# One clearing of the semaphores at the end, and the last stage's first norm made a stage earlier

## The chip, the cores and the metric

The kernel runs on one core of a Trainium2 chip. The metric is the device time of one execution in microseconds. The median of three timed runs of the kernel before is 1267.13 us (1265.65 to 1269.34).

## What is computed

The input is 16 sequences of 256 tokens with 128 features, so 4096 tokens in 32 tiles of 128. Six layers follow one another, each with a residual and a norm of its own in front:

```python
def _layernorm(x, axis=-1, eps=1e-05):
    m = jnp.mean(x, axis=axis, keepdims=True)
    v = jnp.var(x, axis=axis, keepdims=True)
    return (x - m) / jnp.sqrt(v + eps)
...
    x = x + 0.5 * _L0_ffn_ref(_layernorm(x, axis=-1), ...)
    x = x + _L0_attn_ref(_layernorm(x, axis=-1), ...)
    x = x + 0.5 * _L0_ffn_ref(_layernorm(x, axis=-1), ...)
    x = x + 0.5 * _L1_ffn_ref(_layernorm(x, axis=-1), ...)
    x = x + _L1_attn_ref(_layernorm(x, axis=-1), ...)
    x = x + 0.5 * _L1_ffn_ref(_layernorm(x, axis=-1), ...)
    return x
```

`_L0_ffn` routes every token to two of eight experts, `_L0_attn` is differential attention, `_L1_attn` a linear attention whose state is carried along the tokens by a scan. `_L1_ffn` is a feed-forward layer with quantized weights, and it norms its input a second time (mean, `rsqrt(var + EPS)`) and adds its result to that normed input:

```python
        residual = x
        mu = jnp.mean(x, axis=-1, keepdims=True)
        var = jnp.mean(jnp.square(x - mu), axis=-1, keepdims=True)
        h = (x - mu) * jax.lax.rsqrt(var + EPS) * ln_gamma + ln_beta
...
        return residual + 0.5 * z.reshape(residual.shape)
```

So a token of this layer needs two factors from one variance: that of the first norm alone (`r0`, for the residual) and that of both norms together (`r01`, for `h`).

## The kernel before

All 32 tiles of tokens stay on the chip in one array `x` (`all_x` in the trace, features along the free axis). The work is done in groups of four tiles (TG = 4, 512 tokens), so eight groups (NG = 8). Six stages run one after another, each a function that writes the instruction list of every engine by hand: `sorted_moe` ("moe0"), `diff_attention` ("diff"), `sorted_moe` again ("moe1"), `quantized_ffn` ("ffn0"), `linear_attention` ("lin"), `quantized_ffn` again ("ffn1"). Waits and signals between engines are semaphores that the stage allocates through a `Names` object. When a stage ends, three things happen in a row: the end of its block, a barrier of all engines (its line is that of the stage's `with`); then `Names.clear`, which sets the stage's semaphores back on POOL (line 58, a drain and one ranged clear); then a second barrier of all engines (line 59). There are 13 `Names` objects. Five end at the boundaries between stages, with 79, 78, 81, 19 and 23 semaphores; the other eight (ffn1's and those of weights and shared tiles) end one after another at the end of the kernel.

**Start of diff.** POOL issues eight indirect gathers (lines 2039 and 2031) and then makes the first scale `diff_rstd` (2011) by a power on 128x2 values. DVE normalises with it (`diff_xn`, 2535), PE transposes, ACT rounds the result to fp16 (`diff_xT_hi`, 2223).

**Start of moe1.** Part of its rows has been sorted and scattered during diff. POOL scatters the rest group by group (`exp_xs`, line 468), waiting for the row numbers that DVE makes.

**lin's rounds.** A round treats one group in eight steps f = 0 to 7, each for an eighth of the state. For even f DVE multiplies `lin_kv` from PSUM (line 3080), for odd f POOL does it from SBUF (2932). DVE scans (`lin_state`, 3093), POOL multiplies the state with the queries (`lin_y`, 2945), PE projects (`lin_o_ps`, 3164). At f = 5 DVE adds the projected result of the group before to `x` (`add_out`, 3099). Rounds up to the sixth also prepare a later group; the last round prepares nothing, and behind it `add_out` of the last group ends the stage.

**ffn1's start.** For group 0 DVE computes statistics (1539, 1543) and two variances (1546 for both norms, 1548 for the first), POOL raises them to the power -1/2 (`r01` at 1453, `r0` at 1457), DVE normalises four tiles (`ffn_hn`, 1565), PE transposes (1649), ACT and DVE split the result in two fp16 parts (1494, 1571), PE multiplies with the weights (1659 up, 1672 down). Group 1's statistics come behind the split of group 0 on DVE. On POOL an addition of the bias to `x` (1462, 128x512) follows each group's powers; DVE's `ffn_keep` and `ffn_shift` (1557, 1558) make the residual's factors for ACT (1507).

Of the kernel before, what the change touches and what calls it, by code (L numbers as in the profile page):

```python
# [15 lines left out]
P = 128  # L16
# [95 lines left out]
class ExpertWeights:  # L112


    def __init__(self, nc, ctx, w, tiles):
# [4 lines left out]
        nm = Names(nc, ctx, "exp")  # L120
# [48 lines left out]
def sorted_moe(nc, tag, x, ident, neghalf, made, ew, first_layer, fetched_here, x_in=None, later=None, deq=None, ahead=0, fetch=None, begin=None):  # L169
# [75 lines left out]
    with ExitStack() as ctx:  # L245
        nm = Names(nc, ctx, tag)
# [103 lines left out]
        dest_ready = nm.sem("dest_ready")  # L350
        zeroed = nm.sem("zeroed")
        spare_in = nm.sem("spare_in")
# [12 lines left out]
        fetched = [nm.sem(f"fetched{i}") for i in range(YG)]  # L365
        tile_in = [nm.sem(f"tile_in{t}") for t in range(TG)]
        x_added = nm.sem("x_added")
        fetch_used = nm.sem("fetch_used")
        s_g = nm.sem("s_g")
        s_u = nm.sem("s_u")  # L370
        s_act = nm.sem("s_act")
        s_h = nm.sem("s_h")
        s_hi = nm.sem("s_hi")
        s_lo = nm.sem("s_lo")
        s_done = nm.sem("s_done")
        s_added = nm.sem("s_added")
        w1_ready = nm.sem("w1_ready")
        deq_own = nm.sem("deq_own")
# [76 lines left out]
        def _(pool):  # L455
# [810 lines left out]
class Fetched:  # L1266


    def __init__(self, nc, ctx):
        nm = Names(nc, ctx, "fetched")  # L1270
        self.yg = nm.sb("yg", [P, FETCH_RING, TG, 2, P], F32)
        self.come = [nm.sem(f"come{i}") for i in range(FETCH_RING)]
# [2081 lines left out]
```

## Time and profile before

| | us |
|---|---|
| median of three timed runs | 1267.13 |
| the profiled execution, its own time | 1273.58 |
| its span in the trace | 1271.8 |
| PE busy in the span | 1018.7 (80%) |
| DVE busy | 864.3 (68%) |
| ACT busy | 659.8 (52%) |
| POOL busy | 650.0 (51%) |

The stages end at about 230, 773, 971, 1042, 1199 and 1268 us of the span. In the trace a timeline row gives start, duration, engine, line, operation, tile written and tiles read, and in brackets the idle time of the engine before it and what ended that. A row of a line without timeline gives the number of instructions, the shortest, median and longest duration in nanoseconds, and the first and last start. PEclk is the granted clock of TensorE, where 1.00 is 2.4 GHz and 0.50 is 1.2 GHz.

### The profile page before, as it was taken

Reading aid. Unit: us, or ns where it says so; the run is one execution under the profiler, and the core shown is the slowest. Engines: PE = TensorE matmul, PEld = TensorE weight load, DVE = VectorE, ACT = ScalarE, POOL = GpSimd, SP = SyncE. Lnnn points to the kernel's source line nnn. Section 1 sums busy time; section 2 is a strip of 40 time slices with the busy share of each in tenths; the row PEclk is TensorE's granted clock in tenths of the full one; section 3 lists DMA queues with packets and bytes.
Section 4 is the critical chain, followed back from the end, with each engine's and each line's share of the span. In section 5 each row is a group of like instructions: output and inputs, shape, how many; then the busy total and the mean of one; then the engine's idle time right before and its main releaser. Section 6 shows DMA issues by size and latency. Waiting matters only on the chain. (4 is left out here: it accounts for less than half of the span.)

```text
span 1271.8 us, 30703 instructions
## 1 busy us (share of the span) xinstructions
PE 1018.7 (80%) x10960; PEld 750.0 (59%) x10992; DVE 864.3 (68%) x2321; ACT 659.8 (52%) x1248; POOL 650.0 (51%) x697
## 2 busy tenths in 40 slices
PE   3646699778999889898889875787874989999697
PEld 1434588346766666566666644666663765666466
DVE  7645678556887878686868636675556956778672
ACT  4622466536677667576756543343443644444173
POOL 5754300465556576657563334355552316888751
PEclk9868799789999989899999886898887998999999
DMA  8212343134443343334343313422213000000001
GB/s 241 75 45 57 110 115 94 38 56 69 63 58 55 54 67 58 62 57 68 54 62 50 55 27 108 116 74 71 60 36 112 33 1 2 1 1 1 1 26 42
DMA packets 279667, 75.50 MB, mean 59 GB/s; under 512 B 217152, under 2 KB 273504, under 8 KB 279136
## 3 DMA queue, kind: packets, MB, share of 16 engines
q1 hardware_dynamic: 270528, 53.43, 22.2%
q0 software_dynamic: 8992, 20.11, 5.0%
q8 instruction: 92, 1.51, 0.5%
q14 instruction: 55, 0.45, 0.1%
HBM read 28.08 MB, written 24.17 MB: 41 GB/s over the span
## 5 line engine op out<-in xcount | busy, mean ns | idle before, releaser
L2333 DVE TENSOR_REDUCE diff_peak<-diff_s_ps 128x2 f16<-128x384 f32 (+7 forms) x384 | 208.4, 558 | 111.0 <-PE diff_s_ps L2597 74.0
L2183 ACT ACTIVATE diff_prob<-diff_st_ps 128x512 f32<-128x512 f32 x320 | 187.6, 596 | 123.0 <-PE diff_st_ps L2619 97.5
L2619 PE MATMUL diff_st_ps<-diff_qT,diff_k_pair 128*128 128x256 f16 (+3 forms) x1024 | 127.5, 237 | 8.3 <-issue 6.3
L2597 PE MATMUL diff_s_ps<-diff_kT,diff_q_block 128*128 128x32 f16 (+7 forms) x1024 | 132.1, 231 | 1.8 <-issue 1.8
L492 POOL DMA_INDIRECT exp_ys<-moe_y_sb,moe_dest x78 | 78.4, 1005 | 82.9 <-ACT moe_y_sb L578 63.0
L2635 PE MATMUL diff_ot_ps<-diff_prob,diff_v 128*32 128x256 f32 (+3 forms) x2048 | 113.7, 314 | 0.6 <-ACT diff_prob L2183 0.4
L571 ACT ACTIVATE moe_h_hi<-moe_h 128x512 f16<-128x512 f32 x94 | 59.2, 630 | 103.2 <-DVE moe_h L894 90.5
L2594 PE MATMUL diff_s_ps<-diff_mask,diff_ident_bf 128*128 128x64 bf16 (+1 forms) x384 | 79.9, 208 | 31.1 <-DVE diff_peak L2333 20.9
L894 DVE TENSOR_TENSOR moe_h<-moe_act,moe_u_ps 128x512 f32<-128x512 f32 x94 | 64.2, 683 | 45.8 <-remote 20.1
L2945 POOL TENSOR_TENSOR lin_y<-lin_state,lin_qT 128x512 f32<-128x512 f32 x64 | 81.2, 1268 | 15.6 <-DVE lin_state L3093 12.9
L565 ACT ACTIVATE moe_act<-moe_g_ps 128x512 f32<-128x512 f32 x94 | 55.4, 590 | 64.0 <-remote 37.4
L3093 DVE TENSOR_TENSOR_SCAN lin_state<-lin_lam_ps,lin_kv 128x512 f32<-128x512 f32 x64 | 76.6, 1215 | 10.4 <-POOL lin_kv L2932 8.0
L3164 PEld LDWEIGHTS lin_o_ps<-last_lin_wo,lin_y 128*128 128x128 f32 x512 | 65.0, 191 | 26.8 <-POOL lin_y L2945 21.5
L468 POOL DMA_INDIRECT exp_xs<-moe_xh,exp_rows x64 | 64.7, 1010 | 27.8 <-issue 18.3
L3164 PE MATMUL lin_o_ps<-last_lin_wo,lin_y 128*128 128x128 f32 x512 | 70.3, 280 | 10.6 <-POOL lin_y L2945 10.6
L2619 PEld LDWEIGHTS diff_st_ps<-diff_qT,diff_k_pair 128*128 128x128 f16 x1024 | 70.2, 100 | 9.8 <-issue 5.0
L889 DVE TENSOR_TENSOR moe_h_lo<-moe_h,moe_h_hi 128x512 f16<-128x512 f32 x94 | 65.0, 692 | 13.5 <-ACT moe_h_hi L571 9.8
L2615 PE MATMUL diff_st_ps<-diff_mask_T,diff_ident_bf 128*128 128x128 bf16 (+1 forms) x288 | 67.3, 234 | 8.3 <-ACT diff_prob L2183 5.8
L2594 PEld LDWEIGHTS diff_s_ps<-diff_mask,diff_ident_bf 128*128 128x128 bf16 x384 | 38.1, 99 | 59.6 <-DVE diff_peak L2333 44.2
L1140 PE MATMUL moe_g_ps<-moe_xgT,exp_up_hi 128*128 128x256 f16 x312 | 61.0, 291 | 15.3 <-DVE moe_xgT L875 12.9
L2635 PEld LDWEIGHTS diff_ot_ps<-diff_prob,diff_v 128*32 128x32 f32 x2048 | 52.3, 111 | 31.7 <-issue 12.1
L2597 PEld LDWEIGHTS diff_s_ps<-diff_kT,diff_q_block 128*128 128x128 f16 x1024 | 64.5, 101 | 5.8 <-issue 3.8
(438 smaller groups left out, 3035.3 us busy)
## 6 DMA issues: line engine op xcount, KB each, us to landing
moe_xg<-exp_xs SPq DMA_DIRECT2D x78, 130.0 KB, 2.3
diff_q_block<-diff_qT SPq DMA_DIRECT2D x128, 64.0 KB
diff_k_pair<-diff_kT SPq DMA_DIRECT2D x128, 64.0 KB
exp_y_slots<-moe_y_sb SPq DMA_DIRECT2D x39, 128.0 KB, 2.0
diff_v_new<-diff_v_raw SPq DMA_DIRECT2D x64, 64.0 KB
fetched_yg<-exp_ys SPq DMA_DIRECT2D x7, 512.0 KB, 4.0
all_x<-in_x SPq DMA_DIRECT2D x4, 512.0 KB, 5.4
moe_up<-in_w SPq DMA_DIRECT2D x16, 128.0 KB, 3.5
```

The source lines that it names most:

```text
L492: nc.gpsimd.indirect_dma_start(out=ew.ys, out_offset=bass.IndirectOffsetOnAxis(ap=dest[:, s, j:j + 1], axis=0), in_=y_sb[:, s % YR, j], in ...
L889: nc.vector.tensor_tensor(h_lo[:, i % HR], h[:, i % 2], h_hi[:, i % HR], ALU.subtract).then_inc(lo_ready, 1)
L2183: nc.scalar.activation(prob[:, n % RING], st_ps[:, e % 2], ACT.Exp, scale=SCALE).then_inc(exp_ready, 1)
L2333: nc.vector.tensor_reduce(peak[:, half, c0:c0 + n, i], s_ps[:, u % 2, 0:n * wd].rearrange("p (c k) -> p c k", k=wd), op=ALU.max, axis=AX.X ...
L2594: nc.tensor.matmul(out[:, :, wd - QB:], ident_bf[:], mask[:, 0:n], start=True, stop=False, skip_group_check=True)
L2597: last = nc.tensor.matmul(out[:, c], q_block[:, ch, i].rearrange("p r q -> p (r q)"), kT[:, B % 2, ch, 0:wd], start=False, stop=True, skip ...
L2615: nc.tensor.matmul(cols, ident_bf[:], mask_T[:, 0:len(equal)], start=True, stop=False, skip_group_check=True)
L2619: last = nc.tensor.matmul(out[:, at:at + wd], k_pair[:, h % 2, h // 2, i].rearrange("p r k -> p (r k)"), qT[:, C % 3, h // 2, KB * i:S], s ...
L2635: last = nc.tensor.matmul(ot_ps[32 * r:32 * r + 32, half, col:col + wd], v[:, b % 2, i, h], prob[:, (b * EXPS + n) % RING, at:at + wd], st ...
L2945: nc.gpsimd.tensor_tensor(y[:, f % RING], state[:, f % STATES], qT[:, b], ALU.mult).then_inc(y_ready, 1)
L3093: nc.vector.tensor_tensor_scan(state[:, f % STATES], lam_ps[:, b], kv[:, f % RING], 0.0, ALU.mult, ALU.add).then_inc(state_ready, 1)
L3164: last = nc.tensor.matmul(o_ps[:, b, t * P:(t + 1) * P], y[:, f % RING, t * P:(t + 1) * P], wo[:, f], start=(f == 0 and t == 0), stop=(f = ...
```

## The change

Two things are done. First, `Names` takes a list and no longer clears: the barrier at a block's end stays, line 58's clear and line 59's barrier go from all 13 places. The semaphores of moe0 (67 now) are cleared by POOL inside diff, behind the eight gathers and ahead of the first `diff_rstd`; those of diff (78) by POOL inside moe1, between two scatters. All others (70 and 66, in two ranges) are cleared once at the end of the kernel, with one barrier behind. So that enough semaphores are left, the moe stages no longer allocate those that they don't use. Second, the norm of ffn1's group 0 and the statistics of its group 1 move into lin's last round: the tiles and semaphores are a new object `FfnNorm`, handed to both stages as `opening`. They work on groups 0 and 1 of `x`, which lin has finished rounds earlier.

```diff
 class Names:
-    def __init__(self, nc, ctx, prefix):
+    def __init__(self, nc, ctx, prefix, sems):
         self.nc, self.ctx, self.prefix = nc, ctx, prefix
-        self.sems = []
-        ctx.callback(self.clear)
-
-    def clear(self):
-
-        self.nc.clear_and_free_semaphores(self.sems)
-        self.nc.all_engine_barrier()
+        self.sems = sems
...
# sorted_moe, POOL
                 scatter(ahead - 1, EARLY + 1)
+                nc.clear_and_free_semaphores(spent)
                 scatter(ahead)
...
# quantized_ffn, POOL
-            scale_both(0)
-            scale_first(0)
+            if not opened:
+                scale_both(0)
+                scale_first(0)
...
# quantized_ffn, DVE
-            statistics(0)
-            normalise(0)
+            if not opened:
+                statistics(0)
+                normalise(0)
             add_results(1, 0)
             low(0)
             add_results(1, 1)
-            statistics(1)
+            if not opened:
+                statistics(1)
             scales(0)
...
# diff_attention, POOL
                     gather(1, n)
+            if spent:
+                nc.clear_and_free_semaphores(spent)
             scale_of(0)
...
# linear_attention, POOL
+                    if f == 5 and opening and not prepares:
+                        pool.wait_ge(opening.both_var_ready, 1)
+                        nc.gpsimd.tensor_tensor(opening.r01[:, 0], opening.var[:, 0, 0], neghalf[:, 0:TG], ALU.pow).then_inc(opening.r01_ready, 1)
             pairs(pool, group)
+            if opening:
+                pool.wait_ge(opening.var_ready, 1)
+                nc.gpsimd.tensor_tensor(opening.r0[:, 0], opening.var[:, 0, 1], neghalf[:, 0:TG], ALU.pow).then_inc(opening.r0_ready, 1)
...
# linear_attention, DVE
+                    if opening and not prepares and f == 4:
+                        opening_statistics(0)
...
             pairs(dve, group)
+            if opening:
+                opening_normalise()
+                opening_statistics(1)
             add_out(NG - 1, 1)
...
# build
+        nc.clear_and_free_semaphores(sems)
+        nc.all_engine_barrier()
```

`opening_statistics(g)` is the four BN_STATS, four BN_AGGR and two variances of lines 1539 to 1548 on group g; `opening_normalise()` the four instructions of line 1565 on group 0, which wait for `r01`.

DVE from the middle of lin's last round to ffn1's first work. `lin_state` is the scan, `all_x<-all_x,lin_o_ps` is `add_out`, the branches are the change of stage. Before:

```order
L3080 TENSOR_TENSOR lin_kv<-lin_v_ps,lin_kT 128x512
L3093 SCALAR_TENSOR_TENSOR lin_state<-lin_lam_ps,lin_kv 128x512 x2
L3099 TENSOR_TENSOR all_x<-all_x,lin_o_ps 128x512
L3080 TENSOR_TENSOR lin_kv<-lin_v_ps,lin_kT 128x512
L3093 SCALAR_TENSOR_TENSOR lin_state<-lin_lam_ps,lin_kv 128x512 x3
L3099 TENSOR_TENSOR all_x<-all_x,lin_o_ps 128x512
L2852 UNCONDITIONAL_BRANCH
L1520 UNCONDITIONAL_BRANCH
L1539 BN_STATS ffn_stats<-all_x 128x6 x4
L1543 BN_AGGR ffn_mv<-ffn_stats 128x2 x4
L1546 TENSOR_SCALAR ffn_var<-ffn_mv 128x4
L1548 TENSOR_SCALAR ffn_var<-ffn_mv 128x4
```

The same stretch of DVE now, from the scan of f = 3 to the last `add_out`; names with `open_` are the new object's tiles:

```order
L3109 SCALAR_TENSOR_TENSOR lin_state<-lin_lam_ps,lin_kv 128x512
L3120 BN_STATS open_stats<-all_x 128x6 x4
L3124 BN_AGGR open_mv<-open_stats 128x2 x4
L3127 TENSOR_SCALAR open_var<-open_mv 128x4
L3129 TENSOR_SCALAR open_var<-open_mv 128x4
L3109 SCALAR_TENSOR_TENSOR lin_state<-lin_lam_ps,lin_kv 128x512
L3115 TENSOR_TENSOR all_x<-all_x,lin_o_ps 128x512
L3096 TENSOR_TENSOR lin_kv<-lin_v_ps,lin_kT 128x512
L3109 SCALAR_TENSOR_TENSOR lin_state<-lin_lam_ps,lin_kv 128x512 x3
L3134 TENSOR_SCALAR open_hn<-all_x,open_mv,open_r 128x128 x4
L3120 BN_STATS open_stats<-all_x 128x6 x4
```

Group 0's statistics stand ahead of the scan of f = 4, and group 0's normalisation and group 1's statistics between the last scan and the last `add_out`.

POOL from lin's last steps into ffn1, before (`L58 ISA` is the ranged clear):

```order
L2945 TENSOR_TENSOR lin_y<-lin_state,lin_qT 128x512 x2
L2932 TENSOR_TENSOR lin_kv<-lin_v_sb,lin_kT 128x512
L2945 TENSOR_TENSOR lin_y<-lin_state,lin_qT 128x512 x2
L2852 UNCONDITIONAL_BRANCH
L58 ISA
L1449 UNCONDITIONAL_BRANCH
L1453 TENSOR_TENSOR ffn_r<-ffn_var,all_neghalf 128x4
L1457 TENSOR_TENSOR ffn_r<-ffn_var,all_neghalf 128x4
```

and now:

```order
L2955 TENSOR_TENSOR lin_y<-lin_state,lin_qT 128x512 x2
L2960 TENSOR_TENSOR open_r<-open_var,all_neghalf 128x4
L2942 TENSOR_TENSOR lin_kv<-lin_v_sb,lin_kT 128x512
L2955 TENSOR_TENSOR lin_y<-lin_state,lin_qT 128x512 x2
L2965 TENSOR_TENSOR open_r<-open_var,all_neghalf 128x4
L2862 UNCONDITIONAL_BRANCH
L1454 UNCONDITIONAL_BRANCH
L1458 TENSOR_TENSOR open_r<-open_var,all_neghalf 128x4
```

The power for `r01` stands ahead of the last `lin_kv`, that for `r0` behind the last `lin_y`, and the clear is gone.

POOL at diff's start, now (before, the clear stood ahead of the gathers, in a place of its own between the stages):

```order
L2047 DMA diff_prob<-exp_y_slots,exp_places 128x128 x4
L2039 DMA diff_yg<-exp_y_slots,exp_places 128x128 x4
L2077 ISA
L2019 TENSOR_TENSOR diff_rstd<-diff_var,all_neghalf 128x2
L2080 MEMSET diff_k_pack 128x64
```

The clear of moe0's semaphores has moved behind the last gather, directly ahead of the first scale.

## Rows read from the trace of the kernel before

**Rows 1.** Lines 58, 59 at moe0's end: count, ns min/median/max, starts in us.

```profile
L58 POOLq DRAIN  x1: 184/184/184, 230.1 to 230.1; - x1
L58 POOLq EVENT_SEMAPHORE_RANGE_CLEAR  x1: 463/463/463, 230.4 to 230.4; - x1
...
L59 ACTq EVENT_SEMAPHORE  x1: 17/17/17, 231.1 to 231.1; - x1
```

**Rows 2.** The same two lines at lin's end.

```profile
L58 POOLq DRAIN  x1: 77/77/77, 1199.1 to 1199.1; - x1
...
L59 ACTq EVENT_SEMAPHORE  x1: 17/17/17, 1199.6 to 1199.6; - x1
```

**Rows 3.** Line 59 in the last four microseconds of the kernel.

```profile
L59 ACTq EVENT_SEMAPHORE  x8: 17/17/17, 1268.8 to 1271.7; - x8
```

**Rows 4.** Timeline at diff's start: start, us, engine, line, operation, idle before.

```profile
241.80 0.73 POOL L2011 TENSOR_TENSOR diff_rstd<-diff_var,all_neghalf 128x2 f32<-128x2 f32 x1
...
243.72 0.38 ACT L2223 ACTIVATE diff_xT_hi<-diff_m_ps 128x256 f16<-128x256 f32 x1 [0.67 <-PE diff_m_ps L2716]
```

**Rows 5.** diff's end on POOL: a DMA in the timeline, its landing, the drain.

```profile
771.30 0.95 POOL L2136 DMA_INDIRECT exp_xs<-exp_xh,exp_rows  x1 [0.30 <-issue]
...
exp_xs<-exp_xh,exp_rows POOLq DMA_INDIRECT x2, 2.3
...
L58 POOLq DRAIN  x1: 163/163/163, 772.9 to 772.9; - x1
```

**Rows 6.** Timeline in moe1, POOL, the scatter behind the place of the clear.

```profile
788.16 0.95 POOL L468 DMA_INDIRECT exp_xs<-exp_xh,exp_rows  x1 [4.82 <-DVE exp_rows L683]
```

**Rows 7.** Timeline of lin's last round, DVE and POOL.

```profile
1186.38 2.34 DVE L3093 TENSOR_TENSOR_SCAN lin_state<-lin_lam_ps,lin_kv 128x512 f32<-128x512 f32 x2
...
1190.22 2.34 DVE L3093 TENSOR_TENSOR_SCAN lin_state<-lin_lam_ps,lin_kv 128x512 f32<-128x512 f32 x2
...
1194.05 1.22 DVE L3093 TENSOR_TENSOR_SCAN lin_state<-lin_lam_ps,lin_kv 128x512 f32<-128x512 f32 x1 [1.49 <-POOL lin_kv L2932]
...
1192.75 1.27 POOL L2932 TENSOR_TENSOR lin_kv<-lin_v_sb,lin_kT 128x512 f32<-128x512 f32 x1
1193.98 2.64 POOL L2945 TENSOR_TENSOR lin_y<-lin_state,lin_qT 128x512 f32<-128x512 f32 x2
...
1197.87 0.69 DVE L3099 TENSOR_TENSOR all_x<-all_x,lin_o_ps 128x512 f32<-128x512 f32 x1 [2.60 <-PE lin_o_ps L3164]
```

**Rows 8.** Timeline of ffn1's start, DVE, POOL and PE.

```profile
1199.69 0.87 DVE L1539 BATCH_NORM_STATS2 ffn_stats<-all_x 128x6 f32<-128x128 f32 x4 [1.14 <-PEq L59]
...
1201.26 1.01 POOL L1453 TENSOR_TENSOR ffn_r<-ffn_var,all_neghalf 128x4 f32<-128x4 f32 x1 [4.64 <-DVE ffn_var L1546]
1202.24 1.01 POOL L1457 TENSOR_TENSOR ffn_r<-ffn_var,all_neghalf 128x4 f32<-128x4 f32 x1
1202.31 1.11 DVE L1565 TENSOR_SCALAR ffn_hn<-all_x,ffn_mv,ffn_r 128x128 f32<-128x128 f32 x4 [1.05 <-POOL ffn_r L1453]
...
1203.48 1.11 PE L1649 MATMUL ffn_t_ps<-all_ident,ffn_hn 128*128 128x128 f32 x4 [5.64 <-DVE ffn_hn L1565]
...
1206.01 0.61 PE L1659 MATMUL ffn_y_ps<-ffn_hT_hi,deq_fc_hi 128*128 128x512 f16 x1 [1.41 <-DVE ffn_hT_lo L1571]
...
1211.81 0.66 PE L1649 MATMUL ffn_t_ps<-all_ident,ffn_hn 128*128 128x128 f32 x4 [3.06 <-DVE ffn_hn L1565]
```

**Rows 9.** Timeline in ffn1, four normalisations of DVE beside POOL's bias addition.

```profile
1220.38 2.11 DVE L1565 TENSOR_SCALAR ffn_hn<-all_x,ffn_mv,ffn_r 128x128 f32<-128x128 f32 x4
...
1221.14 1.26 POOL L1462 TENSOR_TENSOR all_x<-all_x,last_bias 128x512 f32<-128x512 f32 x1 [0.94 <-ACT all_x L1507]
```

**Rows 10.** Windows: stretch, length, busy PE, PEld, DVE, ACT, POOL, PEclk, DMA.

```profile
970.60:991.00 20.40, 9.68 (x26) 4.15 (x27) 16.84 (x81) 6.79 (x14) 6.16 (x6) 0.50 0.30 96
...
1199.10:1216.58 17.48, 8.63 (x26) 3.42 (x27) 10.47 (x51) 6.72 (x14) 7.19 (x7) 0.71 0.00 0
1216.58:1265.58 49.00, 48.24 (x359) 39.57 (x358) 25.29 (x94) 30.11 (x59) 18.84 (x17) 1.00 0.13 39
```

More of the change, by code:

```diff
@@ L166, in load_consts, with sorted_moe @@
         sp.dma_start(self.own_row[:], w["own_row"]).then_inc(self.consts_in, 16)
-def sorted_moe(nc, tag, x, ident, neghalf, made, ew, first_layer, fetched_here, x_in=None, later=None, deq=None, ahead=0, fetch=None, begin=None):
+def sorted_moe(nc, tag, x, ident, neghalf, made, ew, first_layer, fetched_here, x_in=None, later=None, deq=None, ahead=0, fetch=None, begin=None, sems=None, spent=()):
     w = ew.w
@@ L364, in sorted_moe @@
         y_stored = [nm.sem(f"y_stored{i}") for i in range(YR)]
[L365 to L375, printed above, removed]
+        fetched = [nm.sem(f"fetched{i}") for i in range(YG if fetched_here else 0)]
+        tile_in = [nm.sem(f"tile_in{t}") for t in range(TG if fetched_here else 0)]
+        x_added = nm.sem("x_added") if fetched_here else None
+        fetch_used = nm.sem("fetch_used") if fetched_here else None
+        s_g = nm.sem("s_g") if not ahead else None
+        s_u = nm.sem("s_u") if not ahead else None
+        s_act = nm.sem("s_act") if not ahead else None
+        s_h = nm.sem("s_h") if not ahead else None
+        s_hi = nm.sem("s_hi") if not ahead else None
+        s_lo = nm.sem("s_lo") if not ahead else None
+        s_done = nm.sem("s_done") if not ahead else None
         s_added = nm.sem("s_added")
-        w1_ready = nm.sem("w1_ready")
-        deq_own = nm.sem("deq_own")
+        w1_ready = nm.sem("w1_ready") if deq else None
+        deq_own = nm.sem("deq_own") if deq else None
         block = ctx.enter_context(nc.Block(no_gpsimd_drain=True))
@@ L1313, with __init__ @@
 class LastWeights:
-    def __init__(self, nc, ctx, w):
+    def __init__(self, nc, ctx, w, sems):
         self.w = w
@@ L1372, with __init__ @@
 class NextNorm:
-    def __init__(self, nc, ctx, tiles, done):
-        nm = Names(nc, ctx, "next")
+    def __init__(self, nc, ctx, tiles, done, sems):
+        nm = Names(nc, ctx, "next", sems)
         self.done = done
@@ L3222, in build @@
     NG = T // TG
+    sems, moe0_sems, diff_sems = [], [], []
     with ExitStack() as ctx:
-        nm = Names(nc, ctx, "all")
+        nm = Names(nc, ctx, "all", sems)
         x = nm.sb("x", [P, T + TG, P], F32)
@@ L3266, in _ @@
                     last.load(sp)
-        norm = NextNorm(nc, ctx, T, NG - 2 if "d" in phases else 0)
+        norm = NextNorm(nc, ctx, T, NG - 2 if "d" in phases else 0, sems)
         if "d" in phases:
-            quantized_ffn(nc, "ffn0", x, ident, neghalf, made, dequantized, None, None, experts if fetch else None, fetch, norm)
+            quantized_ffn(nc, "ffn0", x, ident, neghalf, made, dequantized, sems, None, None, experts if fetch else None, fetch, norm)
+        opening = FfnNorm(nc, ctx, "open", sems) if "e" in phases and "f" in phases else None
         if "e" in phases:
-            linear_attention(nc, "lin", x, ident, neghalf, made, last, norm)
+            linear_attention(nc, "lin", x, ident, neghalf, made, last, norm, opening, sems)
         if "f" in phases:
-            quantized_ffn(nc, "ffn1", x, ident, neghalf, made, dequantized, out_tiles, stored)
+            quantized_ffn(nc, "ffn1", x, ident, neghalf, made, dequantized, sems, out_tiles, stored, opened=opening)
         else:
```

123 lines of the change are left out of this document (74 added, 49 removed).

## The prediction

> **What bounds the kernel now.** No engine bounds the whole span, so I read the places that the change touches, each by what ends its wait last. First the two lines of the clear and its barrier. At moe0's end the clear's drain begins at 230.1 and the other engines are let go at 231.1, of which 0.46 us are the ranged clear of 79 semaphores [rows 1]: 1.0 us in which nobody works. The boundaries diff to moe1 and moe1 to ffn0 have 78 and 81 semaphores and read alike, 0.9 us each. At lin's end it is 0.5 us (1199.1 to 1199.6) for 23 semaphores [rows 2], and the same at ffn0's end for 19. At the kernel's end eight of them follow one another: the first lets go at 1268.8, the last at 1271.7, so 2.9 us for seven, 0.41 each, 3.3 us for eight [rows 3]. All 13 together are 7.1 us. They are on the path by construction: behind each the first work of every engine waits for line 59, as DVE does at ffn1's start [rows 8].
>
> Then ffn1's start. From the last `add_out` of lin (1197.87, [rows 7]) to the first multiplication with weights (1206.01) there is a chain of one engine after another: statistics 1199.69, powers 1201.26, normalisation 1202.31, transposes 1203.48 [rows 8]. PE then waits 3.06 us once more, for group 1's normalisation, until 1211.81 [rows 8]. From 1216.58 to 1265.58 PE is busy 48.24 of 49.00 us at the full clock [rows 10], so what is gained ahead of that stretch arrives at the end one for one. In the 17.48 us before it the granted clock is 0.71 on average [rows 10], that is 10.1 us at 1.2 GHz and 7.4 at 2.4 GHz.
>
> Last, the place that takes over the work. In lin's last round POOL is the engine that sets the pace: `lin_kv` 1192.75, two `lin_y` from 1193.98 to 1196.62, back to back, while DVE idles 1.49 us ahead of its last scan and 2.60 us ahead of `add_out` [rows 7].
>
> **Boundaries.** moe0 to diff: 1.0 us go, but the clear comes back inside diff on POOL, behind the last gather, and `diff_rstd` starts there with no idle time [rows 4]: POOL is late already. 67 semaphores by 0.463/79 give 0.39 us, and from the drain's start to the clear's it is 0.3 [rows 1], so `diff_rstd` comes 0.7 later in its stage. DVE, PE and ACT hang on it (ACT's rounding has 0.67 us of idle before it, ended by PE, [rows 4]). Net 0.3. Bounds: 1.0 if other waits hide POOL's clear, and 0.3 - 1.35 = -1.0 if its drain waits until the last gather has landed (2.3 us from its issue, of which the issue itself is 0.95, [rows 5]). Against the second: at diff's end the drain took 0.163 us at 772.9 [rows 5], while a DMA issued at 771.30 would land at 773.6. I take 0.3.
>
> diff to moe1: 0.9 go. The clear of 78 semaphores, 0.3 + 0.46 = 0.8 us, stands where POOL then waits 4.82 us for DVE [rows 6]; that wait hides it, and without it 0.8 would be back. moe1 to ffn0: 0.9. ffn0 to lin: 0.5. Both stages begin with work that waits on line 59 alone. Bounds for each: nothing to the full amount; I take the full amount, 2.3 together, since the barrier's release is what ended the first wait.
>
> Kernel's end: 3.3 us become two drains and ranged clears and one barrier: 0.1 + 70 x 5.9 ns, 0.1 + 66 x 5.9 ns, and a barrier of 1.0 - 0.3 - 0.46 = 0.24 [rows 1], 1.25 us in all. That is a gain of 2.05, of which I take 2.0; bounds 1.6 (drains of 0.3, as at moe0's end) and 2.2.
>
> **lin's last round gets longer.** Four steps. (1) Statistics of group 0 take DVE 1201.26 - 1199.69 = 1.57 us [rows 8], ahead of the scan of f = 4; they move the scan of f = 5 from 1190.22 [rows 7] to about 1191.6 (a little less than 1.57, since DVE waited for PE ahead of it) and its result from 1191.5 to 1192.8. The `lin_y` of f = 5, which POOL began right after the one before, starts about 1.2 us later. (2) The power for `r01` takes POOL 1.0 us [rows 8], ahead of the last `lin_kv`: 1192.75 becomes 1195.0. The last scan starts at 1196.3 instead of 1194.05, and the last `lin_y` runs from 1197.55 to 1198.85, 2.2 us later than before. (3) DVE has finished its last scan at about 1197.4 and should normalise (1.11 us) and make group 1's statistics (1.57), done by 1200.1; PE's projection is done at 1198.85 + 1.2 = 1200.05 (1196.62 to 1197.87 before, [rows 7]). The two would just fit, and `add_out` would be 2.2 us late. (4) But the normalisation runs beside POOL's last `lin_y`. In ffn1 there is a row for just that: four normalisations that take 1.11 us alone [rows 8] took 2.11 when POOL's 128x512 addition began between them [rows 9], ending only when POOL's did; POOL's was not longer. I take the same here: the normalisation stands still until 1198.85, ends at 1199.9, the statistics at 1201.4, and `add_out` starts at 1201.4, 3.5 us late. Bounds 2.2 (no hold) and 4.5 (the power for `r0`, 1.0 us, that POOL starts behind the last `lin_y`, holds it too).
>
> The Trainium skill, page "SBUF — State Buffer", section "SBUF: two separate sides", states that DVE in a two-port mode and GpSimd share one pair of ports as an exclusive lock that the first holds for its whole instruction while the other stands still. The row of the 2.11 us agrees. By the letter of that rule the power would hold DVE as well; the trace doesn't agree: the normalisation of 1202.31 ran beside the power of 1202.24 in its usual 1.11 us [rows 8]. By the rule the sum would be 1.0 us worse, by the row it is as above.
>
> **ffn1's start gets shorter.** Behind `add_out` (0.69) the block's barrier takes 1199.1 - 1198.56 = 0.5 [rows 2, 7], then PE can transpose at once: 1201.4 + 0.7 + 0.5 + 0.1 = 1202.7. From transposes to the first multiplication it is 1206.01 - 1203.48 = 2.5 [rows 8]: 1205.2, a gain of 0.8 against 1206.01 (the boundary's 0.5 is in it). The multiplications of group 0 lasted 1211.81 - 3.06 - 1206.01 = 2.74 us. Group 1's powers now follow from 1202.6 on POOL, two by 1.0 [rows 8], DVE splits until 1205.2, makes the residual's factors and normalises until about 1206.8; PE wants group 1 at 1205.2 + 2.7 = 1207.9. So the wait of 3.06 us goes, and 3.9 are gained. On the clock: if all of PE's 8.63 us of work in that stretch [rows 10] was at half speed, at most 4.3 more can come back. One idle stretch of PE ahead of the transposes stays (1200.05 to 1202.7), the other goes; I take 1.2, nearer to nothing. Together 5.1, bounds 3.9 - 1.0 (longer hold) and 8.2.
>
> **The sum.** 0.3 + 0.9 + 0.9 + 0.5 + 2.0 + 5.1 = 9.7 us. The profiled execution would go from 1273.58 to 1263.9; the median of the timed runs lies 6.45 us (0.5%) below it, and with the same difference 1267.13 becomes 1257.4. A measurement of this kernel tells a change from none at about 0.3%, 3.8 us.
>
> **Rivals.**
> (a) No hold at lin's end: DVE slips its four normalisations in ahead of the last `lin_y` or beside it. 1.3 less, 1256.1. For it: the two start within 0.15 us of each other. Against: the row of 2.11 us.
> (b) The clock doesn't fall at ffn1's start, because PE's idle time there is 2.6 instead of 5.6 us: up to 4.3 - 1.2 = 3.1 more, 1254.3. Against: the wait of 3.06 us was long enough to be followed by some of the 10.1 us at half speed.
> (c) The power holds DVE as well: 1.0 more, 1258.4. Against: the 1.11 beside 1202.24.
> (d) The change does not do what it says: the boundaries' time is only moved, because each stage's first long wait is for a DMA or for POOL's clear (the drain in diff waits for its gathers). Then -1.0 stands for 0.3 and nothing for 2.3: 3.6 less, 1261.0. Against: the first waits end at line 59.
> (e) Slower: the earlier start of ffn1 falls into a long stretch of half clock. ffn0 has one, 20.40 us at 0.50 with PE busy only 9.68 us [rows 10], ended only after PE had become busy. In ffn1 PE is the bound, so every us at half speed costs 0.5. My forecast leaves some 7 us at half; from 7 + 2 x 9.7 = 26 us the gain is gone, from 34 the kernel is slower by 0.3%, and with 40 us it takes 1257.4 + 16.5 = 1274. Against: before, with more idle time, the clock was back for good by 1216.58 [rows 10].
>
> **How the numbers follow.** Forecast 0.41, (a) 0.22, (b) 0.13, (c) 0.05, (d) 0.12, (e) 0.07. Predicted is the likeliest, 1257.4. The range goes from 1252.0, below (a) and (b), to 1262.5, beyond (d) by its unknown drain; what is left out is (e) and the ends of (b) and (d). Faster by over 0.3% (below 1263.3) are the forecast, (a) to (c) and most of (d): 0.91. Within 0.3%: the rest of (d), 0.02, and the shorter stretches of (e), 0.04: 0.06. Slower: 0.03.
>
> **What would show it.** In the profile after: no line 58 and 59 at the boundaries, one pair of clears in the last 1.3 us; in diff a gap of 0.7 us ahead of the first `diff_rstd`; in lin's last round the last `lin_kv` at about 2.2 us later behind the round's start, `open_hn` longer than 1.11 us for four, and `add_out` some 3.5 us later; in ffn1 no wait of PE for group 1's normalisation. The prediction is wrong if the drain in diff takes more than a microsecond, if PE still waits around group 1, or if the granted clock stays at 0.5 for more than 10 us in ffn1.

## The result, and the profile after

The changed kernel was timed three times against the kernel before, 20, 12 and 12 runs: 1258.32, 1262.54 and 1265.47 us in the median against 1266.17, 1272.2 and 1270.9. The ratios are 0.9947 (95% interval 0.9928 to 0.9966), 0.9922 (0.9896 to 0.9948) and 0.9940 (0.9909 to 0.9971): between 0.3 and 1.0% faster, with the best guess near 0.6%, or 7.9 us by the first pair of medians. Forecast were 1257.4 us and a gain of 9.7. One execution scatters by several us (1252.7 to 1266.5 in the first series), so terms of a microsecond can't be read from times. They can be read from the traces by stage.

The table takes, for each profiled execution, the time from the last signal of one stage's end barrier to that of the next (for the kernels that clear between stages, from the end of that clearing's barrier); the last column runs from there to the end of the kernel. The kernels other than before and changed are those of the experiments below; the record counts the profiled execution of the late clear as slow, so its ratio below is that of its five others. moe0, diff and moe1 scatter by 7, 13 and 5 us between kernels whose code there is alike; ffn0, ffn1 and the end repeat within 0.1 to 0.6 us.

| profile | moe0 | diff | moe1 | ffn0 | lin | ffn1 | end |
|---|---|---|---|---|---|---|---|
| before | 229.5 | 541.8 | 197.8 | 69.7 | 156.3 | 68.7 | 3.4 |
| changed | 226.2 | 548.9 | 197.0 | 69.7 | 159.8 | 61.0 | 1.5 |
| changed, second | 229.4 | 539.1 | 196.6 | 69.6 | 159.7 | 60.9 | 1.5 |
| changed, third | 228.4 | 542.9 | 199.9 | 69.7 | 159.8 | 60.9 | 1.5 |
| clears only | 233.6 | 536.3 | 198.2 | 69.2 | 155.5 | 69.3 | 1.5 |
| opening only | 230.3 | 538.6 | 196.9 | 69.1 | 158.1 | 60.9 | 3.8 |
| late clear | 232.7 | 545.2 | 200.7 | 69.2 | 159.6 | 60.9 | 1.5 |
| norm on ACT | 229.3 | 546.3 | 196.6 | 69.5 | 159.8 | 60.9 | 1.5 |
| early norm | 230.8 | 542.9 | 200.3 | 69.3 | 156.4 | 63.1 | 1.5 |
| early norm, second | 227.8 | 536.6 | 199.3 | 69.3 | 156.3 | 63.1 | 1.5 |
| three groups | 230.9 | 538.7 | 195.8 | 69.2 | 155.4 | 59.3 | 1.5 |
| three groups, second | 229.0 | 546.2 | 199.8 | 69.7 | 156.6 | 59.3 | 1.5 |
| one power more | 228.1 | 543.0 | 200.7 | 69.3 | 158.2 | 60.4 | 1.5 |

lin scatters by up to 1.3 us, because its first scan comes 12.1 to 12.4 us behind the stage's start in three profiles (clears only, opening only, the first of three groups) and 13.6 us in all others, whatever the change. Its last round doesn't scatter like that. From that round's first scan (at 1180.72 before, 1180.69 in the changed kernel) to the stage's end it takes 18.33 us before and 21.58 in the changed kernel, and where its code is the same the profiles agree within 0.02, with one exception that opening only shows.

The profiled execution of the changed kernel took 1266.52 us (span 1264.7), 7.06 less than that of before. Its clears, by line (count, ns shortest, median, longest, first and last start): inside diff, inside moe1, and two at the end with the one barrier that is left.

```profile
L2077 POOLq DRAIN  x1: 7115/7115/7115, 230.5 to 230.5; - x1
L2077 POOLq EVENT_SEMAPHORE_RANGE_CLEAR  x1: 398/398/398, 237.7 to 237.7; - x1
...
L495 POOLq DRAIN  x1: 6809/6809/6809, 778.7 to 778.7; - x1
L495 POOLq EVENT_SEMAPHORE_RANGE_CLEAR  x1: 457/457/457, 785.5 to 785.5; - x1
...
L3324 POOLq DRAIN  x2: 134/140/146, 1263.3 to 1263.9; - x2
L3324 POOLq EVENT_SEMAPHORE_RANGE_CLEAR  x2: 392/402/413, 1263.4 to 1264.1; - x2
...
L3325 ACTq EVENT_SEMAPHORE  x1: 17/17/17, 1264.7 to 1264.7; - x1
```

Lines 58 and 59 are gone from the boundaries. The drains of 7.1 and 6.8 us are not work: POOL's sequencer reaches the drain early and holds it while the gathers or scatters in front of it run. What counts is when the ranged clear is through.

Timeline of diff's start in the changed kernel, to be held against [rows 4]:

```profile
236.54 0.94 POOL L2039 DMA_INDIRECT diff_yg<-exp_y_slots,exp_places  x1 [0.30 <-issue]
238.19 0.72 POOL L2019 TENSOR_TENSOR diff_rstd<-diff_var,all_neghalf 128x2 f32<-128x2 f32 x1 [0.71 <-issue]
...
238.95 1.33 DVE L2545 TENSOR_SCALAR diff_xn<-all_x,diff_mv,diff_rstd 128x128 f32<-128x128 f32 x2 [1.05 <-POOL diff_rstd L2019]
239.09 1.11 POOL L2055 TENSOR_TENSOR diff_yg<-diff_yg,exp_gate 128x512 f32<-128x512 f32 x1
...
241.06 0.38 ACT L2233 ACTIVATE diff_xT_hi<-diff_m_ps 128x256 f16<-128x256 f32 x1 [2.24 <-PE diff_m_ps L2726]
```

The gap ahead of `diff_rstd` is the 0.7 that was forecast. Not forecast is the next line: DVE's two normalisations took 1.33 us together and not 0.60, as in the kernel before:

```profile
242.56 0.60 DVE L2535 TENSOR_SCALAR diff_xn<-all_x,diff_mv,diff_rstd 128x128 f32<-128x128 f32 x2 [0.59 <-POOL diff_rstd L2011]
```

POOL's weighting of the gathered rows (`diff_yg`) began at 239.09, while the first of them ran; the second began at 239.21 and ended at 240.28, just behind the weighting.

Timeline of lin's last round and ffn1's start in the changed kernel, the lines that answer to [rows 7] and [rows 8]:

```profile
1193.77 1.01 POOL L2960 TENSOR_TENSOR open_r<-open_var,all_neghalf 128x4 f32<-128x4 f32 x1
...
1194.74 1.26 POOL L2942 TENSOR_TENSOR lin_kv<-lin_v_sb,lin_kT 128x512 f32<-128x512 f32 x1
1195.96 2.66 POOL L2955 TENSOR_TENSOR lin_y<-lin_state,lin_qT 128x512 f32<-128x512 f32 x2
...
1197.17 2.04 DVE L3134 TENSOR_SCALAR open_hn<-all_x,open_mv,open_r 128x128 f32<-128x128 f32 x4
1197.28 3.78 PE L3206 MATMUL lin_o_ps<-last_lin_wo,lin_y 128*128 128x128 f32 x16 [2.26 <-POOL lin_y L2955]
...
1201.10 0.69 DVE L3115 TENSOR_TENSOR all_x<-all_x,lin_o_ps 128x512 f32<-128x512 f32 x1 [0.41 <-PE lin_o_ps L3206]
...
1202.37 1.09 PE L1657 MATMUL ffn_t_ps<-all_ident,open_hn 128*128 128x128 f32 x4 [1.31 <-PEq L2862]
...
1204.87 0.61 PE L1667 MATMUL ffn_y_ps<-ffn_hT_hi,deq_fc_hi 128*128 128x512 f16 x1 [1.42 <-DVE ffn_hT_lo L1577]
```

The four normalisations took 2.04 us beside POOL's last product, about the 2.11 that were forecast. But the line of the last addition says what it waited for: 0.41 us for PE, whose last 16 projections took 3.78 us. The windows of the changed kernel (stretch, length, busy time of PE, PEld, DVE, ACT, POOL, then PEclk, DMA share and GB/s) show why:

```profile
1180.00:1196.00 16.00, 12.28 (x82) 9.20 (x82) 12.48 (x22) 1.79 (x3) 14.66 (x13) 1.00 0.00 2
1196.00:1209.40 13.40, 9.40 (x33) 6.42 (x34) 9.41 (x36) 4.10 (x8) 8.03 (x9) 0.50 0.00 0
1209.40:1216.00 6.60, 6.60 (x45) 4.78 (x44) 3.78 (x18) 6.21 (x13) 3.90 (x4) 0.98 0.00 0
1216.00:1260.00 44.00, 43.76 (x326) 35.70 (x324) 21.71 (x83) 26.64 (x52) 15.65 (x14) 1.00 0.15 43
```

PE had idled 2.26 us for POOL's delayed `lin_y`, and the granted clock was at 0.50, which is 1.2 GHz, from 1196.1 to 1209.7, already inside lin. Before, PE's last eight projections took 1.16 us and the clock was full to the stage's end:

```profile
1196.67 1.16 PE L3164 MATMUL lin_o_ps<-last_lin_wo,lin_y 128*128 128x128 f32 x8 [0.22 <-POOL lin_y L2945]
...
1189.00:1199.00 10.00, 6.61 (x46) 5.13 (x43) 5.24 (x6) 0.60 (x1) 7.39 (x6) 1.00 0.00 0
```

### The profile page after: what moved, and what is told of

The parts are those of the page before. It is cut to its first block and busy times, and to the rows that moved or that the text cites. A ratio compares the mean times of both kernels' runs of the same rounds, so it can differ in the third digit from the quotient of the medians.

```text
span 1264.7 us, 30585 instructions
## 1 busy us (share of the span) xinstructions
PE 1026.6 (81%) x10992; PEld 753.3 (60%) x10992; DVE 865.5 (68%) x2321; ACT 660.1 (52%) x1248; POOL 649.1 (51%) x697
## 5 line engine op out<-in xcount | busy, mean ns | idle before, releaser
L2645 PE MATMUL diff_ot_ps<-diff_prob,diff_v 128*32 128x256 f32 (+3 forms) x2048 | 116.3, 315 | 2.9 <-issue 2.5
L2625 PE MATMUL diff_st_ps<-diff_mask_T,diff_ident_bf 128*128 128x128 bf16 (+1 forms) x320 | 79.9, 250 | 8.5 <-issue 6.2
```

The source lines that it names most:

```text
L2625: nc.tensor.matmul(cols, ident_bf[:], mask_T[:, 0:len(equal)], start=True, stop=False, skip_group_check=True)
L2645: last = nc.tensor.matmul(ot_ps[32 * r:32 * r + 32, half, col:col + wd], v[:, b % 2, i, h], prob[:, (b * EXPS + n) % RING, at:at + wd], st ...
```

## Experiments

Theory: the change is two independent halves; the boundaries and the end give what their barriers took, less the clear in diff; lin's end is set by DVE standing still beside POOL. Two rivals for the 2 us by which the measured gain is smaller than the forecast: diff itself becomes longer (548.9 against 541.8), or that is scatter.

**Clears only** (the changed kernel, ffn1 makes its own first norm):

```diff
-        opening = FfnNorm(nc, ctx, "open", sems) if "e" in phases and "f" in phases else None
+        opening = None
```

> The changed kernel with the first half of the change alone: no clears between stages, but ffn1 makes its own first norm again. Theory: the two halves are separate and add up. lin's stage takes 156.3 us from release to release as before, ffn1's 68.7 us as before, the five boundaries (3.9 us by the trace) and 2.0 us of the kernel's end are gone, and 1.5 us come back at diff's start, where the clear delays the first scale by 0.6 and DVE's second normalisation then stands still beside POOL's weighting. Together 4.4 us faster than before, about 1262. Rival 1: the clear costs diff much more than that (diff took 548.9 us in the changed kernel's profile, 541.8 before); then diff is near 549 here as well and little is gained. Rival 2: these 7 us are scatter between executions; then diff lies anywhere from 540 to 550 with and without the clear.

Measured: 0.9982 of the kernel before (0.9955 to 1.0009; 12 runs). lin 155.5 and ffn1 69.3 us, the end 1.5, and diff 536.3 with the clear ahead of the scale. So the clear doesn't lengthen diff by 7 us, and rival 1 falls. The expected gain of 4.4 us would be a ratio of 0.9965; that lies inside the interval, and so does no gain at all, so the times show neither.

**Opening only** (the clears and barriers between stages as before; `Names` clears again, the clears in diff, moe1 and at the end are taken out):

```diff
 class Names:
-        self.sems = sems
+        self.sems = []
+        ctx.callback(self.clear)
```

> The second half alone: every stage clears its semaphores behind a barrier of its own again, and ffn1's first norm is made in lin's last round (the object of that norm adds one clear of 0.4 us at the end). Theory: lin takes 159.8 us (3.5 longer than before) and ffn1 61.0 (7.7 shorter), so 4.2 - 0.4 = 3.8 us faster than before, about 1262.5. In diff the first scale comes 10.7 us behind the release and the two normalisations take 0.60, as before. Rival 1 (the clear in diff costs 7 us): diff takes 542 here. Rival 2 (scatter): diff lies anywhere from 540 to 550.

Measured: 0.9953 (0.9919 to 0.9986; 12 runs). ffn1 60.9 us: this half alone brings ffn1 down by 7.8. lin took 158.1 and not 159.8. Of the 1.7, 1.3 are its early start (136.9 us to the last round's first scan, 138.2 in the changed kernel), and 0.3 the last round itself, 21.26 in place of 21.58. There PE waited the same 2.26 us, but the clock was full through the first eight projections and at half only in the second eight:

```profile
1192.03 1.16 PE L3209 MATMUL lin_o_ps<-last_lin_wo,lin_y 128*128 128x128 f32 x8 [2.26 <-POOL lin_y L2958]
...
1193.43 2.08 PE L3209 MATMUL lin_o_ps<-last_lin_wo,lin_y 128*128 128x128 f32 x8 [0.24 <-POOL lin_y L2958]
```

DVE was through with its statistics at 1195.44 and PE with the projections at 1195.51, so here the two nearly tie. diff took 538.6 without any clear in it, within the scatter of those with one. In diff's start the two normalisations took 0.60 us, with POOL's weighting behind them:

```profile
243.20 0.60 DVE L2548 TENSOR_SCALAR diff_xn<-all_x,diff_mv,diff_rstd 128x128 f32<-128x128 f32 x2 [0.38 <-POOL diff_rstd L2024]
244.00 1.05 POOL L2060 TENSOR_TENSOR diff_yg<-diff_yg,exp_gate 128x512 f32<-128x512 f32 x1
```

**Late clear in diff** (the changed kernel):

```diff
-            if spent:
-                nc.clear_and_free_semaphores(spent)
             scale_of(0)
...
                     if A is not None:
+                        if spent and A == 0 and u == 9:
+                            nc.clear_and_free_semaphores(spent)
```

> The changed kernel with one thing moved: POOL clears moe0's semaphores not ahead of the first scale but where it waits some 4 us for DVE's first rotary products. Theory: the clear is then hidden; the first scale comes 10.7 us behind the stage's release (11.35 in the changed kernel), the two normalisations take 0.60 together (1.33), ACT's first rounding comes 12.7 behind the release (14.2), so 1.5 us are gained on the changed kernel, about 1256.8. Rival: the clear is hidden where it stands, ACT's three fills set the start of the stage; then the first rounding stays at 14.2.

Measured: 0.9893 (0.9852 to 0.9934; 5 runs). The first scale came 10.66 us behind the stage's release, the normalisations took 0.60 together, ACT's first rounding came 12.56 behind it (14.22 in the changed kernel): theory right, 1.66 us gained at this place. That the ratio is 0.5% below the changed kernel's first one, which is more than that, rests on five runs and on diff's scatter, and the intervals overlap. The early norm, three groups and one power more have the same late clear, with the scale at 10.67 to 10.83 and the rounding at 12.57 to 12.74; the timeline of the early norm shows it:

```profile
242.30 0.74 POOL L2021 TENSOR_TENSOR diff_rstd<-diff_var,all_neghalf 128x2 f32<-128x2 f32 x1
243.08 0.60 DVE L2547 TENSOR_SCALAR diff_xn<-all_x,diff_mv,diff_rstd 128x128 f32<-128x128 f32 x2 [0.59 <-issue]
244.00 1.05 POOL L2057 TENSOR_TENSOR diff_yg<-diff_yg,exp_gate 128x512 f32<-128x512 f32 x1
```

**Norm on ACT.** To see whether DVE's standstill sets lin's end, the normalisation at lin's end goes to ACT:

```diff
# linear_attention, ACT
             pairs(a, group)
+            if opening:
+                a.wait_ge(opening.shift01_ready, 1)
+                for t in range(TG):
+                    last = nc.scalar.activation(opening.hn[:, t], x[:, t], ACT.Identity,
+                                                bias=opening.shift01[:, t:t + 1], scale=opening.r01[:, 0, t:t + 1])
...
# linear_attention, DVE
-                    last = nc.vector.tensor_scalar(opening.hn[:, t], x[:, t], opening.mv[:, 0, t, 0:1], opening.r01[:, 0, t:t + 1],
-                                                   ALU.subtract, ALU.mult)
+                nc.vector.scalar_tensor_tensor(opening.shift01[:], opening.mv[:, 0, :, 0], -1.0, opening.r01[:, 0],
+                                               ALU.mult, ALU.mult).then_inc(opening.shift01_ready, 1)
```

> The changed kernel with one thing moved: the normalisation of ffn1's group 0 at lin's end is made by ACT (with one small product of mean and factor on DVE) instead of by DVE, so that nothing of it stands still beside POOL's last product. Theory: in the changed kernel DVE was done 0.4 us before TensorE's projection, which ran at 1.2 GHz because POOL had been delayed and TensorE had idled; so DVE's statistics end 1.9 us earlier, the last addition waits for TensorE instead, and lin stays at 159.4 to 159.8 us. Rival: DVE's standstill sets lin's end; then lin takes 1.3 us less, 158.5.

Measured (one execution): lin 159.75 us, against 159.77. Its timeline at lin's end:

```profile
1197.17 3.78 PE L3212 MATMUL lin_o_ps<-last_lin_wo,lin_y 128*128 128x128 f32 x16 [2.26 <-POOL lin_y L2957]
1197.24 1.65 ACT L3042 ACTIVATE open_hn<-all_x,open_shift,open_r 128x128 f32<-128x128 f32 x4 [5.77 <-DVE open_shift L3141]
...
1198.51 0.17 DVE L3137 TENSOR_SCALAR open_var<-open_mv 128x4 f32<-128x4 f32 x1
...
1200.99 0.69 DVE L3123 TENSOR_TENSOR all_x<-all_x,lin_o_ps 128x512 f32<-128x512 f32 x1 [2.30 <-PE lin_o_ps L3212]
```

DVE was done at 1198.7 and then waited 2.30 us for PE. The slow projections set lin's end; the standstill is real and was hidden behind them.

**Early norm** (norm on ACT, late clear, and the statistics and powers of the opening spread over rounds with slack; rounds of 17.74 us had been equally long with and without another norm's statistics and power):

```diff
# linear_attention, POOL
-                    if f == 5 and opening and not prepares:
+                    if f == 4 and opening and g == 3:
                         pool.wait_ge(opening.both_var_ready, 1)
...
+                    if f == 4 and opening and g == 6:
+                        pool.wait_ge(opening.var_ready, 1)
...
# linear_attention, DVE
-                    if opening and not prepares and f == 4:
+                    if opening and g == 3 and f == 4:
                         opening_statistics(0)
+                    if opening and g == 6 and f == 4:
+                        opening_statistics(1)
+                    if opening and g == 3 and f == 6:
+                        opening_normalise()
```

Behind the first condition stands the power for `r01`, behind the second that for `r0`, which was made behind the last round; `opening_normalise` is now the small product of mean and factor.

> The changed kernel with the late clear in diff, and with ffn1's first norm spread over rounds of lin in which DVE and POOL have slack: statistics of group 0 and the power for both norms in the fourth round, those of group 1 and the power for the first norm in the seventh, and the normalisation of group 0 on ACT at the end of the last round. Theory: the rounds of 17.74 us do not get longer (rounds with and without another norm's statistics and power were equally long), lin takes 156.3 us again instead of 159.8, ffn1 61 us or, if TensorE's clock stays up through the shorter idle time, down to 59; with 1.5 us from diff's start that is 5 us faster than the changed kernel, about 1253. Rival: what bounds lin's end is something else (TensorE at half clock), and lin stays near 159.

Measured: 0.9895 (0.9863 to 0.9927; 6 runs). lin is back at 156.4 us and its last round at 18.33, so the rounds did hide the work. ffn1 came out at 63.1, not 59 to 61. Timeline of lin's end and ffn1's start, and windows of ffn1's start:

```profile
1196.62 1.16 PE L3213 MATMUL lin_o_ps<-last_lin_wo,lin_y 128*128 128x128 f32 x8 [1.29 <-POOL lin_y L2957]
...
1198.01 1.16 PE L3213 MATMUL lin_o_ps<-last_lin_wo,lin_y 128*128 128x128 f32 x8 [0.22 <-POOL lin_y L2957]
...
1200.48 0.63 PE L1659 MATMUL ffn_t_ps<-all_ident,open_hn 128*128 128x128 f32 x4 [1.31 <-PEq L2864]
...
1207.92 2.10 DVE L1573 TENSOR_SCALAR open_hn<-all_x,open_mv,open_r 128x128 f32<-128x128 f32 x4
...
1208.67 1.26 POOL L1469 TENSOR_TENSOR all_x<-all_x,last_bias 128x512 f32<-128x512 f32 x1 [0.94 <-ACT all_x L1515]
...
1210.07 0.66 PE L1659 MATMUL ffn_t_ps<-all_ident,open_hn 128*128 128x128 f32 x4 [1.91 <-DVE open_hn L1573]
```

```profile
1200.37:1207.37 7.00, 4.56 (x24) 2.23 (x25) 4.58 (x20) 5.33 (x12) 4.89 (x5) 1.00 0.00 0
1207.37:1214.37 7.00, 5.09 (x22) 3.11 (x21) 5.09 (x22) 4.84 (x11) 3.62 (x4) 0.76 0.00 0
```

PE waited 1.29 us for POOL at lin's end, and the transposes took 0.63 us instead of 1.09: the clock stayed at full through lin's end. PE then ran so far ahead that it waited 1.91 us for the third normalisation, which stood still beside POOL's bias addition, and the clock fell after that wait.

The same kernel once more, beside the changed kernel on one chip:

> The changed kernel once more, for a second profile of it and for a comparison on one chip with the other kernels of this call. Theory: lin 159.8 and ffn1 61.0 us as in the first profile, the kernel's end 1.5; moe0 and diff anywhere within some 8 us of their first values. Against the kernel before 0.993 to 0.995. Rival: diff's 548.9 us are the change's doing; then diff is near 549 again.

> The kernel with the norm spread over lin's rounds and the late clear in diff once more, beside the changed kernel on one chip: lin 156.4 and ffn1 63.1 us as in its first profile, so 1.3 us less than the changed kernel from the two, and 1.5 us less at diff's start; ratio to the changed kernel 0.996 to 0.998. If the gain of over 5 us that its first timing suggested is real, the ratio is below 0.996, and something outside these places has become faster.

Measured: the changed kernel 0.9922, the early norm 0.9874 (0.9832 to 0.9916), so about 0.995 of the changed kernel with intervals that overlap. lin and ffn1 account for 1.2 us and diff's start for some 1.8 of the 5.9 between the medians; where the rest comes from, or whether it is there at all, stays open. diff took 539.1 us in the changed kernel this time and 536.6 in the other: the 548.9 of the first profile were scatter.

**Three groups** (early norm, and lin also makes both powers of group 1 and the statistics of group 2; the rings of the norm's tiles get three places):

```diff
# linear_attention, DVE
+                if opening and not prepares:
+                    opening_statistics(2)
                 scan(g, b, NF - 1)
# quantized_ffn, POOL
-            scale_both(1)
-            scale_first(1)
+            if not opened:
+                scale_both(1)
+                scale_first(1)
+            else:
+                scale_both(2)
+                scale_first(2)
```

> As the kernel with the early norm, and lin also makes the powers of group 1 and the statistics of group 2 (in its last round, where DVE waits 1.5 us for POOL's last product), so that ffn1's third normalisation no longer waits for a chain in which POOL's bias addition holds DVE twice. Theory: TensorE's wait of 1.9 us for group 2 goes, with it the 3.2 us at half clock that followed (1.6), lin stays at 156.4 to 156.6, and ffn1 takes 63.1 - 3.5 = 59.6 us; about 6 us faster than the changed kernel. Rival: the wait only moves to group 3, the clock falls then, and ffn1 stays near 63.

Measured: 0.9860 (0.9824 to 0.9897; 6 runs), ffn1 59.3 us. Windows of its start, 7 us each, and the rest:

```profile
1190.67:1197.67 7.00, 4.57 (x24) 2.23 (x25) 3.43 (x15) 5.33 (x12) 3.25 (x3) 1.00 0.00 0
1197.67:1204.67 7.00, 7.00 (x51) 5.47 (x50) 5.58 (x20) 5.75 (x14) 4.53 (x4) 1.00 0.00 0
1204.67:1245.67 41.00, 41.00 (x307) 33.73 (x306) 20.34 (x76) 25.41 (x49) 14.33 (x13) 1.00 0.16 46
```

PE is busy throughout from the second window on, at the full clock. The rival (the wait moves to the next group) falls.

**One power more.** Which delay makes the clock fall at lin's end, that of the statistics on DVE or that of the power on POOL? To the early norm one power on POOL is added where the changed kernel has its own; the result is overwritten later:

```diff
+                    if f == 5 and opening and not prepares:
+                        nc.gpsimd.tensor_tensor(opening.r0[:, 1], opening.var[:, 0, 0], neghalf[:, 0:TG], ALU.pow)
```

> The kernel with the early norm, plus one thing: POOL makes one power more (128x4, its result is overwritten later) ahead of the last product of values and keys in lin's last round, where the changed kernel has one. This measures what that power alone does to TensorE's clock at lin's end. Theory: TensorE's wait for POOL's seventh product grows from 1.3 to 2.3 us, the granted clock falls to 0.5 there as in the changed kernel, so lin grows by 1.0 for the power and about 1.2 for the two projections at half speed, 158.5 us, and ffn1 begins at half clock and takes 61 us. Rival: the fall needs the delayed scan as well (the statistics on DVE ahead of it); then lin takes 157.4 us and the clock stays at 1.00 until ffn1.

Measured (one execution): lin 158.2, 1.8 to 1.9 us longer than the early norm for a power of 1.01. Timeline and window at lin's end:

```profile
1191.75 1.01 POOL L2964 TENSOR_TENSOR open_r<-open_var,all_neghalf 128x4 f32<-128x4 f32 x1
...
1195.27 3.48 PE L3215 MATMUL lin_o_ps<-last_lin_wo,lin_y 128*128 128x128 f32 x16 [2.26 <-POOL lin_y L2957]
1198.78 0.69 DVE L3125 TENSOR_TENSOR all_x<-all_x,lin_o_ps 128x512 f32<-128x512 f32 x1 [3.53 <-PE lin_o_ps L3215]
```

```profile
1193.95:1199.95 6.00, 3.48 (x16) 3.29 (x16) 1.91 (x2) 0.00 (x0) 2.52 (x3) 0.72 0.00 0
```

The power alone does it: PE's wait grows from 1.29 to 2.26 us, the clock falls, and 16 projections take 3.48 us. The rival (it needs the delayed scan as well) falls. Other than expected, the clock was at full again when ffn1 began and fell 1.8 us later. The last comparison on one chip:

> The changed kernel a third time, for the comparison of this call: lin 159.7, ffn1 60.9, the end 1.45 us; 0.992 to 0.995 of the kernel before.

> The kernel with three groups' statistics made in lin once more, beside the changed kernel: lin 155.4 to 156.4, ffn1 59.3 us, so about 5.5 us less than the changed kernel from the two and 1.5 less at diff's start; 0.985 to 0.989 of the kernel before and 0.993 to 0.996 of the changed kernel.

Measured: the changed kernel 0.9940 (0.9909 to 0.9971), three groups 0.9881 (0.9835 to 0.9926). In both comparisons three groups take 0.994 of the changed kernel's ratio; by stages it is 159.8 + 60.9 = 220.7 us against 214.7 and 215.9 for lin and ffn1. Of the first difference, 6.0 us, 1.1 is lin's early start in that profile; the second, 4.8, has none of it. The medians differ by 7.6 us both times (1262.54 against 1254.92, 1265.47 against 1257.87). The intervals of the first pair of ratios (0.9896 to 0.9948, 0.9824 to 0.9897) overlap in one ten-thousandth; in the second pair they overlap more.

## Why the prediction was right, and where its steps were not

**The sum.** 1257.4 us and 9.7 us less were forecast, 1258.3 and 7.9 (by the ratios 7 to 10) measured. By the traces of the first pair: the boundaries ahead of moe1, ffn0 and lin 0.9 + 0.9 + 0.5, since behind the release the stages begin as before (the scatter of [rows 6] 14.3 us behind it against 14.4, lin's first scan 13.6 against 13.6, ffn0's whole time 69.7 against 69.7), the end 3.44 - 1.46 = 2.0, lin and ffn1 with the barrier between them 156.29 + 0.54 + 68.71 - 159.77 - 60.98 = 4.8, forecast 5.1. That is 9.1 before diff's start. What the profiled pair lacks of it lies in moe0 and diff, which scatter by more. The times alone show the whole and the second half; they don't show the first half (clears only), whose terms rest on the traces.

**Clear in diff, forecast +0.3.** The gap was 0.71, as worked out from the 0.463 us for 79 semaphores [rows 1], and the drain didn't wait for landings: the ranged clear began at 237.7, 1.2 us after the last gather was issued, and at diff's end an indirect DMA took 2.3 to land [rows 5]. The step that failed is "net 0.3": the delay put DVE's second normalisation beside POOL's 128x512 weighting, where it took 1.07 us (0.34 before). Without a clear there the two took 0.60 (opening only, late clear). ACT's first rounding therefore came 14.22 us behind moe0's last barrier signal in place of 13.61, 0.6 later instead of 0.3 earlier; the other profiles with this clear have 14.18 to 14.43. By the first maximum that DVE takes in the attention (`diff_peak`) it is 32.3 against 32.6, so the 0.3 is there again, and with the late clear it comes at 30.3 to 30.9. Where the difference between the two points comes from isn't settled. The row for such a standstill stood ahead of the prediction [rows 9]; it was applied at lin's end and not here. The page "SBUF — State Buffer" of the Trainium skill, section "SBUF: two separate sides", has the rule for both, for DVE in a two-port mode: the one that comes second stands still for the other's whole instruction. The rows of diff and of lin's last round agree with it: in both the second normalisation began about 0.1 us behind a 128x512 operation of POOL (239.21 behind 239.09, 1197.41 behind 1197.34) and ended 0.1 behind its end. Which mode DVE was in no row shows.

**Clear in moe1, forecast hidden.** Right: POOL's scatter behind it still waits for DVE, 4.74 us where it was 4.82 [rows 6].

```profile
790.06 0.95 POOL L461 DMA_INDIRECT exp_xs<-exp_xh,exp_rows  x1 [4.74 <-DVE exp_rows L677]
```

**lin's last round, forecast +3.5, measured +3.25, for another reason.** From the last round's first scan (1180.72 before, 1180.69 now) POOL's last product ends 17.93 us on in place of 15.90, `add_out` begins at 20.41 in place of 17.15. The 3.5 us of the table hold another 0.24 from lin's earlier rounds, which scatter without the change. Steps 1 and 2 (statistics and power delay the last `lin_y` by 2.2) were right in kind: 2.03. Step 4, the standstill of DVE, took place (2.04 us), but `add_out` didn't wait for it: DVE was free at 1200.68, and with the norm on ACT, where DVE is free 2 us earlier, lin is as long. The rest, 1.2 us, is PE's 16 projections at half clock: they ended at 1201.06, where with the 1.2 us that lay behind POOL's last product before they would have ended at 1198.62 + 1.2 = 1199.8.

That 1.3 was forecast for the hold and 1.2 came from the clock is luck. The two lie side by side: had the clock stayed full, DVE's statistics would by these numbers have held `add_out` until 1200.7, 0.9 later than PE; that is an estimate, no run has the standstill at full clock, and in opening only the two end within 0.1 us. The prediction had priced the delay of POOL as a delay only. It read the clock in ffn1 and not in the stage whose idle time it lengthened; one power more shows, in one execution, that 1.0 us on POOL is enough for it.

**ffn1's start, forecast 5.1 with lin and the barrier, measured 4.8.** Transposes 0.1 behind the release, 2.50 us from there to the first multiplication (2.5 forecast), 1204.87 against 1205.2, no wait for group 1. Of the clock some 7 us at half were left in ffn1 by the forecast; it was 1209.7 - 1202.3 = 7.4, but they are the tail of a fall that began in lin. Rival (b), no fall, did not come in the changed kernel. The early norm, which gives POOL no extra work in lin's last round, got it at ffn1's start, and three groups throughout.

**Kernel's end**, forecast 2.0, measured 2.0: two clears of 0.39 and 0.41 us.

**Rivals.** (a) fell, the hold is there, though hidden. (c), that the power holds DVE too, fell: 2.04 us is less than the product's and the power's time together, and the normalisations were done at 1199.2 while the power ran until 1199.6. (d) fell: the drain in diff waited for no landing, and the stages behind the removed barriers begin as before. (e) fell: the clock was back for good at 1209.7.

## What to carry to other kernels

Work that is moved under another stage's cover has three prices there: its own time, the instructions of DVE that it brings beside a large one of POOL, and the idle time that it opens on TensorE, after which the granted clock may be at half for many microseconds; rounds that are equally long with and without a step show where the cover is real. The barriers between stages gave back here what they took where the clear left the path (ahead of moe1, ffn0 and lin), and not at diff's start, where the clear stood on POOL's path again. In a kernel whose runs scatter by 1%, terms of 1 us are settled stage by stage in traces.

## What the runs showed of the hardware that was not expected

- A drain that stands behind indirect DMAs of POOL is recorded from the moment when the sequencer reaches it: 7.1 us in diff and 6.8 in moe1, while the engine worked on what stood in front.
- With a wait of TensorE of 2.26 us at lin's end the granted clock fell to 1.2 GHz, with one of 1.29 in the same place it stayed full to the stage's end. The moment differed: in the changed kernel it fell during the wait (1196.1, the wait ended at 1197.28) and was at half until 1209.7, in opening only it fell 1.3 us behind the wait.
- DVE's normalisation stood still beside POOL's 128x512 operations in three stages (1.33 for 0.60 in diff, 2.04 for 1.11 in lin, 2.10 for 1.11 in ffn1), and not beside a power of 128x4 (1.11 for four in [rows 8], 0.33 each in lin).
